# A decoder kernel on one core: earlier set-up loads, five result slots in the expert loop, and half a microsecond of slack in the scheduler

## What is computed

```
x = _layernorm(x + _L0_attn_ref(x, ...))            # 16 heads of 8, rotary positions
x = _layernorm(x + _L0_xattn_ref(x, ctx_1024, ...)) # causal self-attention, attention on the context, a linear block
x = _layernorm(x + _L0_ffn_ref(x, ...))             # activations quantized to 8 bits, int8 weights
x = _layernorm(x + _L1_attn_ref(x, ...))            # 0.6 attention + 0.4 of a local window of +-3
x = _layernorm(x + _L1_xattn_ref(x, ctx_1024, ..., mask, ...))
x = _layernorm(x + _L1_ffn_ref(x, ...))             # 8 experts, best one of each token
x = _layernorm(x + _L2_attn_ref(x, ...))            # norm, masked attention, context attention, gelu block
x = _layernorm(x + _L2_xattn_ref(x, ctx_1024, ...))
x = _layernorm(x + _L2_ffn_ref(x, ...))             # 16 experts, best two
x = _layernorm(x + _L3_attn_ref(x, ...))            # attention along the batch dimension
x = _layernorm(x + _L3_xattn_ref(x, ctx_1024, ...))
x = _layernorm(x + _L3_ffn_ref(x, ...))             # a shared expert and 31 experts, best three
```

## Time and profile before

| | us |
|---|---|
| median of 3 runs | 2639.15 |
| lowest, highest | 2636.06, 2651.93 |
| profiled execution, its own time | 2615.75 |
| its span in the profile | 2613.9 |

### The profile page before, as it was taken

One profiled execution on the slowest core, in us unless ns is written; L12 is line 12 of the kernel. 1 busy time (PEld: TensorE's weight loads), 2 busy tenths in 40 slices (PEclk: granted clock), 3 DMA queues, 4 the chain that ended last, 5 costly groups with the idle time before them and its releaser, 6 DMA issues. The chain is left out here.

```text
span 2613.9 us, 43617 instructions
## 1 busy us (share of the span) xinstructions
PE 2080.8 (80%) x15046; PEld 1028.6 (39%) x15046; DVE 1549.0 (59%) x3259; ACT 1145.6 (44%) x2217; POOL 770.5 (29%) x943
## 2 busy tenths in 40 slices
PE   3799999987799999668999898864958776795373
PEld 1123355543333344554554444434922222333252
DVE  5678766657878843365665555342567776437134
ACT  0267765562177765122654766631423221161031
POOL 4201102113411101333112112115406667203663
PEclk9779999988799999677997998976978887796576
DMA  3410011110111000342011001005910000100265
GB/s 124 167 57 26 26 39 32 27 28 1 49 34 29 20 17 14 106 160 61 26 33 32 20 12 31 24 36 179 326 39 0 1 0 0 43 16 18 78 188 150
DMA packets 135005, 148.44 MB, mean 57 GB/s; under 512 B 29366, under 2 KB 119926, under 8 KB 133635
## 3 DMA queue, kind: packets, MB, share of 16 engines
q1 hardware_dynamic: 97604, 104.58, 13.8%
q10 hardware_dynamic: 29376, 24.97, 3.1%
q0 software_dynamic: 7808, 16.10, 1.7%
HBM read 72.61 MB, written 26.99 MB: 38 GB/s over the span
## 5 line engine op out<-in xcount | busy, mean ns | idle before, releaser
L1538 DVE TENSOR_REDUCE maxima<-psM 128x2 f32<-128x1024 f32 (+4 forms) x640 | 677.6, 1080 | 343.9 <-PE psM L1209 135.5
L1402 ACT ACTIVATE probs<-psE 128x512 f32<-128x512 f32 (+2 forms) x1248 | 698.8, 584 | 397.8 <-PE psE L1232 188.3
L1232 PE MATMUL psE<-q_stack,k_stack 53*128 53x512 bf16 (+3 forms) x1152 | 371.8, 360 | 43.8 <-ACT probs L1402 34.1
L1209 PE MATMUL psM<-k_stack,q_stack 51*128 51x512 bf16 (+3 forms) x1280 | 350.8, 349 | 8.7 <-DVE maxima L1538 6.9
L1686 POOL TENSOR_SCALAR pool_t<-mean_var 128x4 f32<-128x4 f32 x60 | 15.0, 251 | 655.0 <-DVE mean_var L1463 651.3
L1232 PEld LDWEIGHTS psE<-q_stack,k_stack 53*128 53x128 bf16 x1152 | 98.0, 94 | 242.6 <-ACT probs L1402 160.7
L2237 POOL DMA_INDIRECT by_token<-probs,y_slot x148 | 141.7, 957 | 130.8 <-DVEq L2181 121.0
L1209 PEld LDWEIGHTS psM<-k_stack,q_stack 51*128 51x128 bf16 x1280 | 101.5, 97 | 163.7 <-issue 86.2
L2013 ACT COPY probs<-psE 128x128 f32<-128x128 f32 x148 | 39.4, 266 | 282.0 <-PE psE L1942 176.6
L1143 PE MATMUL psM<-masks_bf,ident_bf 64*128 64x128 bf16 (+2 forms) x832 | 153.1, 266 | 5.1 <-DMA k_stack<-k_parts 4.9
L1252 PE MATMUL psB<-probs,values 128*32 128x256 f32 (+3 forms) x1728 | 154.8, 430 | 1.7 <-ACT probs L1402 1.2
(11 more groups left out here) (475 smaller groups left out, 3805.2 us busy)
## 6 DMA issues: line engine op xcount, KB each, us to landing
q_stack<-q_parts SPq DMA_DIRECT2D x432, 64.0 KB
values<-experts_dram SPq DMA_DIRECT2D x40, 514.0 KB
values<-experts_dram SPq DMA_DIRECT2D x79, 128.5 KB, 2.1
k_stack<-k_parts SPq DMA_DIRECT2D x156, 64.0 KB
hid<-experts_dram SPq DMA_DIRECT2D x15, 514.0 KB
work<-experts_dram SPq DMA_DIRECT2D x15, 514.0 KB
sorted<-hid ACTq DMA_DIRECT2D x7, 1024.0 KB, 10.7
c_values<-sorted ACTq DMA_DIRECT2D x78, 65.0 KB
```

The costliest lines, as they stand in the source:

```text
L1209: out, len(heads), keys, lo, max_mask(c, t), lambda i, to, start, stop: nc.tensor.matmul(to, q_stack[lo:lo + R_MAX, job.a % Q_SLOTS, pair_ ...
L1232: lambda h, to, start, stop: nc.tensor.matmul(to, ks[lo:lo + R_END, pairs[h], k * P:k * P + c.kn], q_stack[lo:lo + R_END, job.a % Q_SLOTS, ...
L1402: nc.scalar.activation(probs[0:c.kn, m % 2, heads[0]:heads[-1] + 1, q0:S], psE[0:c.kn, n % 2, 0:len(heads) * (S - q0)].rearrange("p (h q) ...
L1538: nc.vector.tensor_reduce(top, psM[:, at:at + len(banks), 0:per * keys].rearrange("p b (h k) -> p b h k", h=per), AX_X, ALU.max, negate=Tr ...
```

## The change

It has three parts.

1. **Set-up.** `PACKED` is put into another order, so that what the first attention needs, and the small columns that DVE needs in the set-up, stand in the first 2327 columns. SP loads these in the set-up; the other 6968 columns are loaded by a DMA which ACT issues as its last act there, counted by a new semaphore `pack_loaded`. In segment 1 PE waits for it ahead of the first `q`, `k`, `v` or `out` of a job that has no rotary positions. That is `v` of the context attention of u0, PE's rows 14 to 16 of the order before. The bias row is loaded as 128 × 22 (2743 floats and 73 of padding), split on 128 partitions, and brought into its three rows by three DMAs on ACT's queue, each of 128 pieces of 22 bf16 values. ACT also issues the four DMAs on `ident_bf` and `masks_bf`. `k_stack` and `q_stack` are filled as half as many fp32 elements, whose bits are two bf16 ones. POOL's order becomes zeros, `k_stack`, `kc_stack`, `c_values`, `q_stack`, `hid`, and SP waits for three of POOL's casts and not four. Clearing `probs` moves to DVE's start.
2. **Result slots.** `Y_SLOTS` is 5, with two more semaphores.
3. **Scheduler.** `ready()` adds 0.5 us to each hop from another engine to a small PE item. The engines' orders, the fills' places and their numbers follow from it.

The diff, without the lists of names:

```diff
 PACKED = (
...
+    [("ident", P), ("rot", P), ("cos", S), ("sin", S)] + [(f"L0a_{w}", D) for w in ("wq", "wk", "wv", "wo")]
...
+FIRST_W = PACK_AT["L0s_wq"][0]
+TWO_ONES = 1.0 + 0x3F80 / 2.0 ** 23
...
+SLACK = {("PE", task) for task in ("q", "k", "v", "rq", "rk", "rows", "gather", "local", "turn", "out", "back", "hidden")}
...
-                begin_at[engine, item] = max([ended[a] + hop(a[0], engine) for a in after[engine, item]], default=0.0)
+                slack = 0.5 if (engine, item[0]) in SLACK else 0.0
+                begin_at[engine, item] = max([ended[a] + hop(a[0], engine) + (slack if a[0] not in ("ISSUED", engine) else 0.0)
+                                              for a in after[engine, item]], default=0.0)
...
-        y_slot = sb("y_slot", [P, 3, 1], I32)
+        y_slot = sb("y_slot", [P, 5, 1], I32)
...
+            per = ROW_W // P
+            row_f = work[:, 3, 0:per]
+            row_high, row_mid, row_low = (work[:, 3, a:a + per // 2].bitcast(BF16) for a in (64, 128, 192))
 
             @block.sync
             def _(sp):
-                sp.dma_start(row_f, io["rows"]).then_inc(loads, 16)
+                sp.dma_start(row_f, io["rows"].rearrange("o (p w) -> (o p) w", p=P)).then_inc(loads, 16)
...
-                sp.dma_start(pack[:], io["pack"]).then_inc(loads, 16)
+                sp.dma_start(pack[:, 0:FIRST_W], io["pack"][:, 0:FIRST_W]).then_inc(loads, 16)
...
-                sp.wait_ge(cast, 4)
+                sp.wait_ge(cast, 3)
...
-                sp.wait_ge(halves_cast, 2)
-                for both in (ident_bf, masks_bf):
-                    for lo in (0, 64):
-                        sp.dma_start(both[lo:lo + 64, 1, :], both[64 - lo:128 - lo, 0, :]).then_inc(rolled, 16)
-                sp.wait_ge(row_parts, 1)
-                sp.dma_start(rows[1:2, :], row_mid).then_inc(rolled, 16)
-                sp.dma_start(rows[2:3, :], row_low).then_inc(rolled, 16)
-                sp.wait_ge(rolled, 16 * 6)
                 sp.wait_ge(loads, 16 * 12)
 
             @block.gpsimd
             def _(pool):
                 nc.gpsimd.memset(zeros_bf[:], 0.0).then_inc(cast, 1)
+                nc.gpsimd.memset(k_stack[:].rearrange("p k h n -> p (k h n)").bitcast(F32), TWO_ONES).then_inc(cast, 1)
+                nc.gpsimd.memset(kc_stack[:], 1.0).then_inc(cast, 1)
+                nc.gpsimd.memset(c_values[:], 0.0).then_inc(cast, 1)
+                nc.gpsimd.memset(q_stack[:].rearrange("p s h n -> p (s h n)").bitcast(F32), TWO_ONES).then_inc(cast, 1)
                 nc.gpsimd.memset(hid[:], 0.0)
-                nc.gpsimd.memset(k_stack[:], 1.0).then_inc(cast, 1)
-                nc.gpsimd.memset(kc_stack[:], 1.0).then_inc(cast, 1)
-                nc.gpsimd.memset(q_stack[:], 1.0).then_inc(cast, 1)
-                nc.gpsimd.memset(c_values[:], 0.0).then_inc(cast, 1)
...
             @block.scalar
             def _(act):
                 act.wait_ge(loads, 16 * 12)
+                act.wait_ge(halves_cast, 2)
+                for both in (ident_bf, masks_bf):
+                    for lo in (0, 64):
+                        act.dma_start(both[lo:lo + 64, 1, :], both[64 - lo:128 - lo, 0, :]).then_inc(rolled, 16)
+                act.wait_ge(row_parts, 1)
+                for n, part in enumerate((row_high, row_mid, row_low)):
+                    act.dma_start(rows[n:n + 1, :].rearrange("o (p w) -> o p w", p=P), part).then_inc(rolled, 16)
+                act.wait_ge(rolled, 16 * 7)
+                nc.scalar.dma_start(pack[:, FIRST_W:PACK_W], io["pack"][:, FIRST_W:PACK_W]).then_inc(pack_loaded, 16)
...
             @block.vector
             def _(dve):
                 me = Own(dve, own)
                 nc.vector.memset(values[:], 1.0)
+                nc.vector.memset(probs[:], 0.0)
...
                 dve.sem_inc(row_parts, 1)
-                nc.vector.memset(probs[:], 0.0)
...
+                        if rest and task in ("q", "k", "v", "out") and not (job.att and job.att.rope):
+                            pe.wait_ge(pack_loaded, 16)
+                            rest = False
...
-            W_SLOTS, X_SLOTS, Y_SLOTS = 5, 7, 3
+            W_SLOTS, X_SLOTS, Y_SLOTS = 5, 7, 5
```

More of the change, by code:

```diff
@@ L2497, in build @@
             Job("att", u, L1c, "std", xt[:, u]),
-        ] for u in range(B)], [0, 1, 2, 3] * 5), linear, meanwhile=clear_sorted_rows)
+        ] for u in range(B)], [0, 1, 2, 3] * 5), linear, meanwhile=clear_sorted_rows, rest_needed=True)
         routed_experts(1, E1, K1, "experts1")
@@ L2602 @@
     r["scorer"] = a["L2_attn_scorer_logits"][0]
+    r["pad"] = np.zeros(73)
     def experts(w1, w2):
```

26 lines of the change are left out of this document (12 added, 14 removed).

## The result

The changed kernel took 2652.16 us (median of 20 runs, 2642.47 to 2659.39), the kernel before 2638.74 beside it (20 runs, 2617.56 to 2659.93). The ratio is 1.005, 95% interval 1.0033 to 1.0067: slower by 13 us where I forecast 31 us less.

The account below looks back on a forecast made before the run. Each stage was taken to have its own limit: a set-up chain, TensorE's work and waits in the segments, hops in layer 3's routed experts. −16 − 5.5 − 1.5 − 6 − 2 = −31 us gave a 2608 median (2585 profiled), range 2586 to 2636.

Parts of the forecast that it names:

- Set-up: Before the first matmul: smaller load and split bias row gain 16 us, ends 13 and 18; first matmul at 24.2.
- rival c: Segment 1, `v` of the context attention: the rest of `pack` is late, up to +10 us, 2618; chance 0.09.
- Slots: Expert loops: five result slots gain 4.5 us in the third loop and 1 in the second, sum 5.5.
- Scheduler: Order and fills in segments 1, 2 and 3: −1.5, −6 and −2 us.
- Place two: Segment 1, VectorE's `yt` behind 33 fills: with 2 fills there its wait goes, −7.2 us.
- Place one: Segment 1, `max` step behind fills: 79 fills where 33 stood, +4.8 us, ends 0 and +12.4.
- Small waits: Segment 1, TensorE: small waits are exchanged for others, 0 us with −5 as the end.
- nothing else has to give: Segment 1, where `yt` waited: VectorE is the busier engine and late next, so the −7.2 us counts whole.
- Segment 2: Start of segment 2: 28 fills in TensorE's wait for keys hold the clock, −6 us, ends −15 and +6.
- Segment 3: Segment 3: 35 fills fewer, mostly in waits that stay, −2 us, ends −6 and +3.
- (a): Segments: the order gives nothing, fills only change places with waits, 2618; chance 0.33 together with slots giving nothing.
- (b): Segments 1 and 2: 129 added fills land on the path, +37 us, total 2655; chance 0.08.

Follow-up runs that it names:

- mend (d): Changed kernel with ScalarE's ten clearing DMAs issued behind the copy of `max_rows`, not ahead of it: 0.9994 of before.
- (c): Changed kernel without any fills: 0.9971 of before, segment 1 1031.4 us, segment 2 569.0 us.
- back hops: Changed kernel with slack for gather, local, turn, out, back and hidden only: 0.9911 of before, segment 1 1023.2 us.
- fourth group: On one chip: before, the changed kernel (0.9983), and it with slack only for q, k, v, rq, rk, rows (0.9972) or only for the other hops (0.9911).
- third group: On one chip against before: changed kernel 1.0057; with two mends 0.9992; without slack and fills 0.9965; with slack in segment 2 alone 0.9943.
- two mends: Changed kernel with clears behind the `max_rows` copy (0.9994) or fill blocks taking time in the model (0.9975); both together 0.9992 of before.

## Why the prediction was wrong, step by step

**Set-up: right.** Forecast 16, measured 15.9 in the profile and 15 alone (0.9942). The terms were good: the loads landed at 13.98 for 13.2, the bias row took 0.8 for 1.0 us, the landing 1.6 for 2. What the Trainium skill says in DMA: Bandwidth & Descriptors, section Specifications, of transfers under 512 bytes (that a DMA engine does a read-modify-write) brought no cost beyond my 2 us: three DMAs of 44-byte pieces were down 1.6 us after their issue. No run has the same bytes in large pieces, so its price stays unknown. The rest of `pack` (rival c) cost nothing.

**Slots: the mechanism right, the term too small.** I took half of the 9.6 us between 106.6 and the floor of 97.0. On most chips the loop went all the way: 97.3 to 98.3 us in ten kernels, against 106.6 to 110.4 with three slots, and the third stage shrank from 250.7, 253.7 and 254.3 to 241.2. Alone, the slots gave 13 us (4 to 21) for my 5.5. In the profile with the stage of 241.2 us VectorE still waited on slots for 21.6 us (38.6 in the earlier trace rows):

```profile
DVE y_slot L2187 <- DMA by_token<-probs,y_slot: 21.6, 26, 1.6
```

The argument that kept me from the full 9.6, that other waits would take the slots' place, was the weak one. My mark "under 10 us of slot waits" was wrong in itself: the loop was at its floor with 21.6 us of them.

**Scheduler: this step failed.** I had −1.5, −6 and −2, −9.5 in all; measured alone it is +33 us (21 to 46), where my ends were −33 and +25. Three profiles of each kernel give +32.9 for segment 1 (means of 1042.0 and 1009.1), +8.7 for segment 2 (582.6, 573.9) and +3.9 for segment 3 (137.0, 133.1). They add up to more than 33, which shows how much single profiles vary: only segment 1 is clear of that. By their parts:

- *Place two, −7.2:* right, the wait is gone.
- *Place one, +4.8:* about right for the wait. In the three profiles of each kernel it is 8.2 to 11.4 us for 2.9 to 4.1, and it goes with the double block in the other runs too. How much of it reaches the segment's end is not shown, as the lags are mixed.
- *Small waits, 0, and "nothing else has to give":* wrong. I read two places of a table in which many items had moved and took the rest as an exchange of waits for waits. Idle time was indeed exchanged (84 to 86 us for 88 to 92), but busy time was not. It rose by 37 us (three means, 957 and 919). The fills' own time explains 8 us of that (67.50 for 266 recorded against 59.10 for 202). Most of the rest is work done at half clock: 176 us at half clock instead of 128, 48 us in which work of 24 us at full clock fits. Whether the lost clock is the cause or only goes with it is open. Without fills the order of before has 218 us at half clock and is no longer for it (1007.1), and there the slack's order costs 14 us of idle time and 10 of busy time.
- *The clears:* not in my sum at all. The diff moves no DMA, but the first `o_copy` carries ten, and what stands behind it on ScalarE had changed. In the eight profiles with the copy of `max_rows` behind the clears TensorE's waits there are 13.2 to 14.9 us together, in those with the order of before 10.3, with mend (d) 8.5. So the new place cost 3 to 5 us of waits. I should have looked at what stands behind each long block of issues in either order.
- *Segment 2, −6 with fills that hold the clock:* wrong sign. The fills waited 11.04 us for a bank that ScalarE had not read. I had priced them as if they could start where the wait started; even so they ended 3.2 us behind the keys (1195.9 to 1192.73) and not 2. In all seven profiles with the slack in all hops and its fills they waited 10.1 to 11.0 us, and the first `max` step came 36 to 39 us into the segment, where it comes at 25 to 28 in the order of before and in (c). The rule on the throttled default state (the Trainium skill, TensorE: Matmul & The Clock Gate, section What's actually happening) is borne out (the clock rose from 0.50 to 1.00 under the fills), but the wait had already cost the clock by then, and 10 us after its rise it was down again.
- *Segment 3, −2:* 139.6, 139.6 and 131.8 us against 132.0, 135.4 and 131.8; the sign is open.

With no fills the slack's order still costs segment 1 24 us (1031.4 against 1007.1, one profile each), more than the fills add to it (1042.0 against 1031.4). So the order of the items is the larger part, and the fills the smaller, as far as single profiles tell. Part of the order's cost is the clears; the 5 us behind 689 us of the segment go with the back hops and have no row that names them. That part stays open.

**Rivals.** (a) did not come out on either chip (2618 forecast; +13 us on the first, −0.2% on that of the fourth group): it had the order at nothing, where the slack took about as much as set-up and slots gave. (b) had the right sign of the schedule and nearly its size (33 us for its 37), but by the wrong mechanism: the fills' own time was 8 us of it in segment 1. That its total, 2655, lies 3 us from the measured 2652 is luck besides, since the slots lost in the first profile (a third stage of 268.1 for 250.7 us) where (b) has them winning 5.5. The condition I set for "slower", that the schedule costs over 21 us, was met, and on the chip of the fourth group the kernel is still not slower, as set-up and slots had given 25 where they were run without the slack.

**What depends on the chip.** On the chip of the third group four kernels with five slots took 122 to 124 us in the third loop, and the changed kernel 127 in its first profile. The row that differs is SyncE's reading of an expert's number, in the changed kernel on that chip and on the one of the fourth group:

```profile
L1879 SPq TENSOR_LOAD <-q_stack x67: 3/266/716, 2510.8 to 2619.1; - x67
```

```profile
L1879 SPq TENSOR_LOAD <-q_stack x72: 262/269/398, 2492.9 to 2581.2; - x72
```

Up to 716 ns against 398 at most, and likewise for its register operations (717 against 159). In all five profiles with the long loop 30 to 44 of SyncE's register operations in this stage took over 400 ns, in all other profiles none. In the first profile of the changed kernel GpSimd's scatters come some at 1.26 and then one at 2.8, with a wait put down to VectorE's sequencer:

```profile
2501.07 0.96 POOL L2250 DMA_INDIRECT by_token<-probs,y_slot  x1 [0.30 <-issue]
2503.85 0.96 POOL L2250 DMA_INDIRECT by_token<-probs,y_slot  x1 [1.83 <-DVEq L2194]
2505.11 0.96 POOL L2250 DMA_INDIRECT by_token<-probs,y_slot  x1 [0.30 <-issue]
```

That is 25 us, 1% of the kernel, and more than what 1.0057 and 0.9983 differ by (0.7%). How SyncE's slow operations lead to these gaps, and what makes them slow, is not shown. Whether three slots are as slow there is open too: the kernel before has no profile on that chip. That before took 2634.67 us beside it, and 2615.13 to 2623.0 on four others, argues that part of it comes with any number of slots, but does not show it.

## What to carry to other kernels

Leave a list scheduler's order alone unless all of it is checked: a constant in its hops moves every queue, and part of the cost sits where it meets what the model doesn't know, here ten DMA issues tied to one copy and a fill that needs a bank. Judge such an order by the stage's length in several profiles: idle time hardly moved in the changed kernel (86 for 88 us), and time at half clock rose by 60 to 90 us without fills at no cost in length. And compare two ratios only when both kernels ran on the same chip: two mends looked 0.6 and 0.75% good against a ratio from another chip, and together they were worth 0.65%.

## What the runs showed of the hardware that I had not expected

- A stage of the same program differed by 24 us between two chips (265.0 us against 241.2), with single SyncE register operations of up to 717 ns where the other had 159.
- In segment 1 no profile shows fills to be worth anything: without them 218 to 239 us were at half clock instead of 113 to 188, and the segment was no longer than with them (1031.4 for 1035 to 1049 in the changed kernel, 1007.1 for 1000 to 1015 in the order of before). In segment 2 the order of before took 583.1 us without fills and 570 to 580 with them, the slack's order 569.0 without and 578 to 589 with them; a gain of fills there is not shown either.
- Fifteen us of set-up and 13 us of slots added up to 25, but stage lengths that each looked best in one profile (1006 and 561) did not appear together: 1010 and 572.
